# Reordering the fill and the drain of a software pipeline: spiking attention, layer norms and an expert layer on one core

## What is computed

```python
def lif_step(v, x_t):
    v = v + (x_t - v) * TAU_INV      # 0.5
    s = spike(v - V_TH)              # 1.0 where v >= 1
    v = v * (1.0 - s)
    return v, s
# attention: r, k, v are spikes of x@Wr, x@Wk, x@Wv
h = h * DECAY + k * v;  y = r * h
x1  = layernorm(x + y @ Wo.T)
s1  = lif_scan(x1 @ W1.T + b1)                  # 1024 features
ffn = lif_scan(s1 @ W2.T + b2)                  # 256 features
x3  = layernorm(x + layernorm(x1 + ffn))        # two norms in a row
gates = softmax(x3 @ Wg + bg), two largest of 8, renormalised
out = layernorm(x3 + sum over the two chosen experts of gate * (x3 @ We + be))
```

## Time and profile before

| | |
|---|---|
| median of 3 runs | 978.52 us (977.82 to 978.61) |
| the profiled execution | 978.42 us, span 976.6 us |
| TensorE busy | 930.1 us (95%) |
| VectorE busy | 917.0 us (94%) |
| ScalarE busy | 611.3 us (63%) |
| GpSimd busy | 572.1 us (59%) |
| beats 3 to 6, start of the LIF scans | 61.56, 81.25, 103.36, 127.38 us |
| first steady scan | 149.69 us |
| scans of beats 34 and 35 | 904.13 and 929.67 us |

### The profile page before, as it was taken

One profiled execution on the slowest core, in us unless ns is written; L12 is line 12 of the kernel. 1 busy time (PEld: TensorE's weight loads), 2 busy tenths in 40 slices (PEclk: granted clock), 3 DMA queues, 4 the chain that ended last, 5 costly groups with the idle time before them and its releaser, 6 DMA issues.

```text
span 976.6 us, 20766 instructions
## 1 busy us (share of the span) xinstructions
PE 930.1 (95%) x6586; PEld 864.8 (89%) x6586; DVE 917.0 (94%) x3680; ACT 611.3 (63%) x1392; POOL 572.1 (59%) x731
## 2 busy tenths in 40 slices
PE   8988889999999999999999999999999999999975
PEld 7878789999999999999999999999999999788764
DVE  7899998999999999999999999999999999989875
ACT  6665455667666666676666667766666676555542
POOL 1221226766666776666677766666776666664542
PEclk9999999999999999999999999999999999999988
DMA  8643224445656555456555544665555455547754
GB/s 280 156 87 66 55 55 87 103 104 109 120 122 126 110 109 106 99 122 119 120 120 108 109 104 103 120 127 123 112 106 110 97 119 108 105 92 137 139 103 97
DMA packets 59437, 109.71 MB, mean 112 GB/s; under 512 B 6592, under 2 KB 6592, under 8 KB 59328
## 3 DMA queue, kind: packets, MB, share of 16 engines
q0 software_dynamic: 37728, 68.71, 41.1%
q1 hardware_dynamic: 16992, 31.30, 9.7%
q10 hardware_dynamic: 4608, 8.39, 2.2%
HBM read 31.29 MB, written 8.39 MB: 41 GB/s over the span
## 4 chain that ended last, share of the span: by engine, by line
PE 72%; DVE 17%; issue 3%; DMA 3%; ACT 3%; POOL 2%; SPq 0%; POOLq 0%; DVEq 0%; ACTq 0%
PE ps_e L420 29%; PE ps_proj L420 10%; PE ps_proj L510 10%; PE ps_proj L495 9%; PE ps_proj L518 5%; DVE U L984 4%; PE ps_attn L420 3%; DVE V L991 3%; PE ps_zx L474 2%; DMA odd_sum<-term 2%; DVE stats L1063 2%; DVE h L1033 1%; PE ps_attn L474 1%; DVE s L1456 1%; POOL s L1528 1%
## 5 line engine op out<-in xcount | busy, mean ns | idle before, releaser
L984 DVE SCALAR_TENSOR_TENSOR U<-V,U 128x256 f32<-128x256 f32 (+4 forms) x576 | 228.3, 396 | 3.9 <-ACT U L725 1.9
L991 DVE SCALAR_TENSOR_TENSOR V<-U 128x256 f32<-128x256 f32 (+4 forms) x576 | 224.6, 390 | 1.9
L420 PE MATMUL ps_e<-we_hi,x_hi 128*128 128x512 f32 (+1 forms) x618 | 220.6, 357 | 0.1
L420 PE MATMUL ps_e<-we_lo,x_hi 128*128 128x512 f32 (+1 forms) x618 | 215.7, 349 | 0.0
L420 PE MATMUL ps_e<-we_hi,x_lo 128*128 128x512 f32 (+1 forms) x618 | 215.1, 348 | 0.0
L1514 POOL TENSOR_SCALAR veps<-mv 128x2 f32<-128x2 f32 x128 | 47.0, 368 | 271.4 <-DVE mv L1069 269.4
L1528 POOL TENSOR_SCALAR s<-U 128x256 fp32r<-128x256 f32 x208 | 192.7, 982 | 16.3 <-DVE V L991 16.3
L764 ACT ACTIVATE term<-ps_e,gate 128x256 f32<-128x256 f32 x361 | 155.4, 475 | 40.9 <-PE ps_e L420 40.7
L725 ACT ACTIVATE U<-ps_proj,cst 128x256 f32<-128x256 f32 x320 | 135.2, 479 | 68.9 <-PE ps_proj L518 60.4
L510 PE MATMUL ps_proj<-x_hi,w_hi 128*128 128x256 f32 x512 | 133.2, 282 | 0.9 <-ACT x_hi L743 0.9
L710 ACT ACTIVATE U<-ps_proj 128x512 f32<-128x512 f32 x96 | 57.2, 597 | 121.1 <-PE ps_proj L420 121.1
(11 more groups left out here) (125 smaller groups left out, 2359.5 us busy)
## 6 DMA issues: line engine op xcount, KB each, us to landing
odd_sum<-term POOLq DMA_DIRECT2D x94, 256.0 KB, 3.3
acc<-term POOLq DMA_DIRECT2D x93, 256.0 KB, 3.7
xt<-x_T SPq DMA_DIRECT2D x33, 256.0 KB, 3.0
xa<-x_tok SPq DMA_DIRECT2D x32, 256.0 KB, 3.2
xb<-cst SPq DMA_DIRECT2D x32, 256.0 KB, 2.3
xb<-x_tok POOLq DMA_DIRECT2D x32, 256.0 KB, 6.1
xt<-x_hi POOLq DMA_DIRECT2D x31, 256.0 KB, 4.3
out<-res ACTq DMA_DIRECT2D x31, 256.0 KB, 2.0
```

Of the source, the lines that this page charges most:

```text
L420: mm = pe.matmul(dst, lhs, rhs, start=(i == 0), stop=(i == n - 1))
L984: v.scalar_tensor_tensor(out=U[:, s, t, c0:c1], in0=V[:, c0:c1], scalar=0.5, in1=U[:, s, t, c0:c1], op0=ALU.mult, op1=ALU.add).then_inc(do ...
L991: v.scalar_tensor_tensor(out=V[:, c0:c1], in0=u, scalar=THRESHOLD, in1=u, op0=ALU.is_lt, op1=ALU.mult).then_inc(done, 1)
```

## The change

- **Filler products.** In beats 2 to 6 TensorE begins with 12 filler products, after x1 of the chunk before is read.
- **Spike tiles.** In beats 3 to 6 GpSimd takes six of the eight: four at its beat's head, two behind the power of ln1. VectorE keeps two, in slot 1.
- **Slots of the fill.** ln1_sum, its statistics and its shift go three slots later, x1_low too in beats 3, 4 and 6 and one slot in beat 2. The low part of Wo goes from slot 31 of beat 3 to slot 16.
- **Beat 34.** It gets a slot table of its own, `LAST_S`, and TensorE and ScalarE put the transpose of x3 and its reading behind expert fill 5 instead of 4.
- **Tail.** In `tail` one LIF half follows each piece of other work. `fin_stage(b, 0)`, the sum with the bias, goes from behind gate stage 3 to behind the statistics of ln3; the order holds for beat 36 too, which has no LIF.
- **Beat 37.** Expert adds 2, 3 and 4 come first, then `fin_stage` 1 to 3; `fin_stage` 4 comes behind add 5, and `fin_stage` 0 behind the gates.

```diff
+BRIDGE_Y = 12
-FILL = dict(z_sum=-1, y=(-1,) * 5, spikes_h1=-1, fin_sum=-1,
+FILL = dict(z_sum=-1, y=(-1,) * 5, spikes_h1=1, fin_sum=-1,
             gate=(4, 5, 6, 7, 8, 10, 10, 11, 11, 12, 24, 26), add_e0=(13, 14),
-            ln1_sum=1, ln1_stats=(2, 3), ln1_aggr=4, ln1_norm=7, x1_low=17,
+            ln1_sum=4, ln1_stats=(5, 6), ln1_aggr=7, ln1_norm=10, x1_low=17,
             ln2_stats=(0, 0), ln2_aggr=1, ln2_scale=(5, 6), ln2_add=9,
             ln3_stats=10, ln3_aggr=11, ln3_shift=15, x3_low=28,
-X1_LOW = {1: 23, 3: 19, 4: 19, 6: 15}
+X1_LOW = {1: 23, 2: 18, 3: 22, 4: 22, 6: 18}
+LAST_S = dict(DRAIN, gate=(-1, -1, -1, -1, 2, 4, 5, 6, 7, 8, 17, 18), ln2_stats=(0, 1), ln2_aggr=2, ln2_scale=(3, 5),
+              ln2_add=10, ln3_stats=12, ln3_aggr=14, fin_sum=16, add_e0=(20, 22), ln3_shift=27,
+              fin_add=29, fin_stats=30, fin_aggr=31, x3_low=31)
     def dve_spikes(self):
-        return FK if self.edge else 0
+        return FK if self.late else 2 if self.early else 0
 # TensorE, beat
+                if b.early and b.k > LAG_Y:
+                    pe.wait_ge(x1_ready, b.value(DK, LAG_Y))
+                    bridge(ps_attn[:, 0, :], BRIDGE_Y)
-                        if part == 4 and b.has(LAG_Z) and b.late:
+                        if part == (5 if Beat(b.k + 1).tail else 4) and b.has(LAG_Z) and b.late:
                             x3_T(b)
...
 # VectorE, tail
+                halves = iter([half for t in range(STEPS) for half in ((0, t), (1, t))] if b.lif() else [])
+                membrane_reset = lif_part(b, *lif_columns(b)) if b.lif() else ()
+                def lif_next(n):
+                    for which, t in itertools.islice(halves, n):
+                        membrane_reset[which](t)
+                dve.wait_ge(zT_done, b.value(1, LAG_Z, 1))
+                for j in range(TILES):
+                    bn_stats(1, j, ps_zx[:, j, :], ln2_steps)
+                    lif_next(1)
+                bn_aggr(b, 1, ln2_steps, LN2_STEPS, LAG_Z, 2)
+                lif_next(1)
+                for step in range(4):
+                    gate_stage(b, step)
+                    lif_next(1)
...
+                bn_aggr(b, 2, ln3_steps, LN3_STEPS, LAG_Z, 2)
+                lif_next(1)
+                fin_stage(b, 0)
+                lif_next(1)
+                for j in range(TILES):
+                    add_e0(b, j)
+                    lif_next(1)
+                mean_shift(b, 2, ln3_steps, LAG_Z)
+                lif_next(1)
...
+                fin_stage(b, 3)
+                lif_next(2 * STEPS)
+                x3_low(b)
 # VectorE, last_experts
+                for fill in (2, 3, 4):
+                    add_expert(b, fill)
+                for step in (1, 2, 3):
+                    fin_stage(b, step)
                 total = acc[:, b.slot(LAG_M, 2)]
...
                 add_expert(b, 5)
+                fin_stage(b, 4)
 # VectorE, side
-                if b.k == LAG_S and slot == 2 * STEPS - 1:
+                if b.k == LAG_S and slot == STEPS:
 # GpSimd, beat
-                    for part in range((FK - b.dve_spikes) // 2):
+                    for part in range(2 if b.early else (FK - b.dve_spikes) // 2):
                         spikes_h1(b, part)
...
                     reciprocal_std(b, 0, ln1_steps, LN1_STEPS, LAG_Y, 5)
+                if b.has(LAG_S) and b.early:
+                    spikes_h1(b, 2)
```

More of the change, by code:

```diff
@@ L19 @@
+import itertools
 from contextlib import ExitStack
@@ L1272, in next_sum, with tail @@
                 z_sum(Beat(b.k + 1), 1)
-            def ln2_finish(b):
+            def tail(b):
+                halves = iter([half for t in range(STEPS) for half in ((0, t), (1, t))] if b.lif() else [])
[12 more added lines that the diff above has]
+                    lif_next(1)
+                after(ln2_steps, LN2_STEPS, LAG_Z, b, 4)
+                for j in range(TILES):
+                    ln2_scale(b, j)
+                    lif_next(1)
+                for step in range(4, 10):
+                    gate_stage(b, step)
+                    lif_next(1)
                 after(ln2_steps, LN2_STEPS, LAG_Z, b, 6)
@@ L1277, in ln2_finish @@
                 dve.wait_ge(xb_ready, b.value(16, LAG_Z, 16))
-                ln2_add(b, 0)
-                ln2_add(b, 1)
+                for j in range(TILES):
+                    ln2_add(b, j)
+                    lif_next(1)
                 after(ln2_steps, LN2_STEPS, LAG_Z, b, 8)
-                bn_stats(2, 0, w[:, 0, :], ln3_steps)
-                bn_stats(2, 1, w[:, 1, :], ln3_steps)
+                for j in range(TILES):
+                    bn_stats(2, j, w[:, j, :], ln3_steps)
+                    lif_next(1)
@@ L1283, in ln2_finish @@
                 bn_aggr(b, 2, ln3_steps, LN3_STEPS, LAG_Z, 2)
[L1285 to L1302, removed]
-                    gate_stage(b, step)
[L1304 to L1307, removed]
-                for step in range(4, 10):
-                    gate_stage(b, step)
-                ln2_finish(b)
-                add_e0(b, 0)
-                add_e0(b, 1)
-                gate_stage(b, 10)
-                gate_stage(b, 11)
-                mean_shift(b, 2, ln3_steps, LAG_Z)
@@ L1316, in tail @@
+                lif_next(1)
+                fin_stage(b, 0)
+                lif_next(1)
+                for j in range(TILES):
+                    add_e0(b, j)
+                    lif_next(1)
+                mean_shift(b, 2, ln3_steps, LAG_Z)
+                lif_next(1)
+                for step in (10, 11):
+                    gate_stage(b, step)
+                    lif_next(1)
                 fin_stage(b, 1)
+                lif_next(1)
                 fin_stage(b, 2)
+                lif_next(1)
@@ L1318, in tail @@
                 fin_stage(b, 3)
-                lif_to(STEPS)
+                lif_next(2 * STEPS)
                 x3_low(b)
@@ L1325, in last_experts @@
             def last_experts(b):
-                for step in range(4):
+                for step in range(10):
                     gate_stage(b, step)
                 fin_stage(b, 0)
-                for step in range(4, 10):
-                    gate_stage(b, step)
                 add_e0(b, 0)
@@ L1360, in side @@
                 state_in_lif(b, slot)
-                at = STEADY if not b.edge else FIRST_Y if b.k == LAG_Y else FILL if b.early else DRAIN
+                at = STEADY if not b.edge else FIRST_Y if b.k == LAG_Y else FILL if b.early else LAST_S if Beat(b.k + 1).tail else DRAIN
                 if b.has(LAG_Z):
```

7 lines of the change are left out of this document (removed).

## The result

| | before | after |
|---|---|---|
| median of the runs | 978.57 us | 986.75 us (985.75 to 989.95, 4 runs) |
| ratio, 95% interval | | 1.0092 [1.0078, 1.0106] |
| profiled execution, its span | 978.42, 976.6 us | 989.95, 988.1 us |
| start of the first steady scan, from the first LIF instruction | 137.4 us | 145.8 us |
| z transpose of beat 34 to the end | 75.0 us | 74.1 us |

A forecast was written before the change was run, and what follows sets the result against it. TensorE bounds the untouched steady middle and lies only 0.67 us off the fill's path, where VectorE looks like the bound. Fill +4.7 and drain −2.05 gave +2.65 us: 981.2 us against the median, range 975.5 to 985.0.

The forecast's parts named there:

- They cancel: Rival: half the stretch, clock held in beats 5 and 6, fill +2.5 against drain −2.5, 978.5 us; chance 0.25.
- VectorE stays the bound: Rival: VectorE bounds through beat 6, so the fill gains 1.3 us; with the drain's 2.05, 975.2 us; chance 0.20.
- Exclusion of the ports: Rival: VectorE stands for GpSimd's whole tile times in the fill, 17.5 us; 990 or more; chance 0.05.
- does not take: Rival: fill's clock falls as before, attn's stand in beat 4 stays, 1.2 us lost; 982.4, within the forecast's range.
- filler: Fill, TensorE: 12 products, 1.45 us; delay x1 in beat 2, z transpose in beat 6; cover attn's hole in beat 4.
- spike tiles: Fill, beats 3 to 6: six tiles leave VectorE, 1.22 us a beat; after 0.9 of stretch a beat keeps 0.3.
- later slots of ln1 and x1_low: Fill: the shift comes later behind y in beat 5, +1.55 us; x1_low later in beat 6, +2.35.
- clock in beat 6: Fill: larger hole before the x1 transpose; at half clock w2 ends after x1_low, 0 to 1.4 us, taken as 0.7.
- beat 34: Drain: later shift holds ScalarE and expert fill 5; z transpose +1.5 us, +0.5 for the clock: +2.0.
- late bias sum: Beats 35 and 36: it holds GpSimd's odd add and ln3's power; about 1.1 us, then logits 1.3 later.
- rest of the tail: Drain: beat 35's LIF in bubbles, clock held at z transpose of beat 36 (−1.6), beat 37's odd-DMA stand shortened (−1.15).
- stretch: Fill: VectorE's instructions run longer beside GpSimd's tiles, 0.15 us a tile, 0.9 for six; bounds 0 and 0.22 a tile.

The follow-up runs named there:

- fill_only: The change's fill (later slots, x1_low, tiles, filler) with the drain of before; ratio 1.0089, 988.3 us.
- slots_only: Kernel before with only ln1's later slots and the later x1_low; tiles stay on VectorE, no filler, drain as before; 984.65 us, ratio 1.0070.
- tiles_only: Kernel before with only the six spike tiles of beats 3 to 6 moved to GpSimd; 982.61 us, ratio 1.0042.
- holes_filled: Kernel after plus 24 filler products in beats 5 and 6 between the r/k/v products and x1's transpose; 984.89 us, ratio 1.0072.
- tail_only: Kernel before with the interleaved LIF of the last beats and new order of the last experts, beat 34 as before; 976.05 us, ratio 0.9972.
- tail_bias_early: As tail_only, with the bias sum put back behind the gate's fourth step; 971.83 us, ratio 0.9934.
- drain_only: The whole change of the drain with the fill of before; 977.81 us, ratio 0.9994.

## Why the prediction was right and wrong

**Direction.** The fill loses more than the drain gains: right. *They cancel* and *VectorE stays the bound* are out: VectorE does stand for the z transpose at the head of beat 6, 2.56 us, and the first steady beat is later, not earlier. *Exclusion of the ports* is out by size, as shown. That the clock falls in the fill as before (*does not take*) was too mild: in fill_only's trace it was low for 24 us of the fill, 10 before.

| term | predicted | measured |
|---|---|---|
| filler | +1.2 in beat 2, +1.45 in beat 6, −1.2 for attn in beat 4 | +2.1 alone; within the whole beat 6 +2.3, beats 2 to 5 no cost seen |
| spike tiles | −0.3 a beat | +4.1 alone |
| later slots of ln1 and x1_low | +1.55 in beat 5, +2.35 in beat 6 | +6.8 alone, 5.0 (3.0 to 7.0) within the whole |
| clock in beat 6 | +0.7 (0 to 1.4) | 2.0 (−0.2 to +4.1), for beats 5 and 6 |
| **fill** | **+4.7**, +1 to +6.5 | **+8.7** |
| beat 34 | +2.0 | +2.2 (0.7 to 3.7) |
| late bias sum | +1.1 in beat 35, +1.3 in beat 36 | +3.7 (2.0 to 5.4) |
| rest of the tail | −6.45 (−3.7 − 1.6 − 1.15) | −6.5 |
| **drain** | **−2.05** | **−0.6** |

(The tail's −3.7 is my −2.6 for beat 35 without the 1.1 of the bias sum. The fill's parts alone make 13.0 us and together 8.7: they overlap.)

The fill's sum can be followed mark by mark, in us later than before, from the first LIF instruction:

| mark | predicted | after |
|---|---|---|
| end of y, beat 4 | +0.9 | +3.0 |
| end of y, beat 5 | −0.6 | +1.5 |
| x1's transpose, beat 5 | +0.95 | +4.0 |
| z transpose, beat 6 | +2.4 | +5.5 |
| first product with x1_lo, beat 6 | +4.7 | +10.2 |

Of the 5.5 us missed in this trace 2.1 arise up to y of beat 5, 0.9 with the later norm of beat 5 and 2.3 in beat 6.

**The later norm against the tiles: the step that failed most.** The failed step is the exchange of six tiles for three LIF halves, which I took to be even or nearly so. Within the whole the slots cost 5.0 us (3.0 to 7.0), where 3.9 were priced with the tiles' relief already taken off, and the tiles with the filler of beats 2 to 5 cost 2.3 (0.2 to 4.3), where a gain of 0.6 was booked. I set three LIF halves against six tiles and found them even in beats 3 and 4; in beat 3 the shift came 7.7 us behind the end of y for 6.0. I took the shift of beat 5 to come 8.95 us after y for 7.39: it came 9.75 us after the end of y for 7.31, and 9.76 in slots_only, where the tiles are still in their place: the tiles' 1.22 us, which I subtracted, bought nothing. In after VectorE reached the statistics only 0.63 us earlier and stood 0.43 us there for TensorE, and stretch took the rest. In beat 6 the same shift went from 7.80 us to 10.56 (slots_only) and 12.58 (after, with the filler's 1.45 and the 0.50 for the power). For beat 6 I had priced x1_low and not the shift, which there too is on the path: x1's transpose came 14.1 us behind y for 9.1. Three slots are not three halves, since other work lies in them (ln2_scale, the gate) and had to be passed as well.

**Spike tiles.** The stretch was near (0.20 for 0.15). The relief was booked in full although VectorE used none of it: instead of 0.3 us gained in each of beats 3 and 4, y of beat 5 came 1.5 us late in tiles_only. That is the whole loss of its traced run, which was the fastest of the five (+1.6). This doesn't reach the median's +4.1; the runs of tiles_only have a mean clock of 0.986 against 0.989 of before, which at half speed is 2.8 us at most. Where the rest arises is not settled.

**Filler.** Beat 6's was right in place and, within its interval, in size, and so was what was late next. Beat 2's 1.2 us came as predicted (y of beat 3 at +1.0), but the slots would have brought them alone. In beat 3 y lost 2.0 us against a forecast gain of 0.3, and the gain of 1.5 in beat 4 came. The loss in beat 3 is no work of the slots alone (0.2 in slots_only, 0.9 in tiles_only); the low clock in after between 70 and 80 us may have a part in it, which no run separates.

**Clock.** I took 0.7 for beat 6. In after w2 took 6.41 us for 4.02; holes_filled gave 2 us back for beats 5 and 6 (−0.2 to +4.1), and then waited for VectorE. If mis-sized, it is the smaller part of the miss.

**Drain.** Hole before fill 5: 2.6 predicted and 2.57 found. z of beat 35: 920.2 predicted and 920.3 found (laid on before by the z transpose of beat 34). No drop of the clock at z of beat 36, as forecast. The trace of after loses 1.6 us from the z transpose of beat 34 to that of 35 (1.5 predicted, and 0.5 for the clock), gains 1.1 to the next (3.1 predicted, less 0.5 for the clock) and 1.4 from there to the end (1.45 predicted). Two steps failed, both behind the bias sum. I followed its chain to ln3's power and VectorE and stopped before the gate's stages 10 and 11 and TensorE's turned gates; for beat 35 I priced it at 1.1 us, and it costs 1.8 (16.2 us from z to z in tail_only, 14.4 in tail_bias_early). And the hole that it makes there can lower the clock: 2.1 us in the trace of after where I had put 0.5, so that z of beat 36 came at 938.7 for 936.6. With the clock held, in drain_only and tail_only, beat 35 took 16.2 us, near my 16.4. drain_only had its low clock in beat 34 (20.0 us for 17.1): in which hole it falls differs between these two traces, and two allowances of 0.5 us were too small for it.

## What to carry to other kernels

- An instruction moved by n slots moves by all the work in these slots. Time that leaves an engine counts as a gain only if the next instruction really starts earlier: look for the stand that takes its place, and lay ends and starts of named instructions of both traces side by side, not busy shares.
- Follow a delayed wait to an engine that is the bound, across every queue: here bias sum, GpSimd's DMA, power, shift, gate stage, TensorE. Stopping two links early priced the late bias sum at 2.4 us, where it measured 3.7 (2.0 to 5.4), and hid the best edit of the case, one line moved.
- Two changes that delay the same point don't add, and undoing one of them can show nothing; run each alone and each undone.

## What the hardware showed that was not expected

- Filling TensorE's holes raises the granted clock and need not save time: mean clock 0.9937 for 0.9906 and 972.86 us for 971.83.
- A hole of the same length in the same place was followed by a low clock in one kernel's trace and not in two others': 2.86 us ahead of the turned gates of beat 35 in after, then 0.5 for 6.8 us; 2.84 and 2.92 us in drain_only and tail_only, then 1.00.
- VectorE's instructions beside GpSimd's tiles are longer by parts of a tile: y 0.89 us for 0.42, a state 0.47 for 0.18. Over beats 3 to 6 it comes to 0.14 (tiles_only) to 0.20 us (after) for each tile, nearly as much as the tile costs on VectorE itself. The tiles too are longer there: their median is 1.02 us in after, up to 1.52, where I took 0.93.
- GpSimd's veps has 0.57 us in the record where it starts during the issue of a DMA (945.98 above) and 0.22 where it starts behind it, but from the start of the issue to the end of veps it is 1.14 us there and 1.15 here (920.56 to 921.71 in tail_bias_early): the longer record is no loss of time.
